# First layer of a four-layer graph network: softmax on 16 steps at once, weighted one-hots, one masking product, and every engine one turn behind the one that feeds it

## The chip, the cores and the metric

One core of one Trainium2 chip runs the whole network in one program. The metric is the device time of one execution in microseconds (us), median of several. A core has TensorE (matrix products; TensorE's weight loads are counted apart), VectorE, ScalarE and GpSimd, a queue SP that issues DMAs, 16 DMA engines, an on-chip memory SBUF and the accumulators of TensorE, PSUM, in 8 banks. The engines run their own instruction streams and wait for each other by semaphores.

## The reference

6250 nodes with 128 features, 100,000 edges sorted by destination, four message-passing layers, each followed by a residual and a layer norm:

```
edge_index = [src, dst]
x = layernorm(x + GAT(x))        # first layer
x = layernorm(x + CF(x, edge_attr_128))
x = layernorm(x + GCN(x))
x = layernorm(x + GIN(x))

GAT:  h = x @ W;  a_s = h @ att_src;  a_d = h @ att_dst      (self-loops are added to the edges)
      e = leaky_relu(a_s[src] + a_d[dst], 0.2)
      e = exp(e - segment_max(e, dst)[dst])
      out = segment_sum(h[src] * e / segment_sum(e)[dst], dst) + bias
CF:   f = ssp(edge @ We1 + be1) @ We2 + be2                   (ssp = softplus - log 2; the edge filter)
      agg = segment_sum((node @ Wn)[dst] * f, src);  node + ssp(agg @ W2 + b2) @ W3 + b3
GCN:  segment_sum(dinv[src] * dinv[dst] * (x @ W.T)[src], dst) + b
GIN:  relu((segment_sum(x[src], dst) + x) @ W1 + b1) @ W2 + b2
```

## The kernel before

The nodes are cut into 49 blocks of 128, the sorted edges into 832 steps of 128, none of which spans two blocks. Four steps (`GRP`) are a turn (a "tick" in the code), so there are 208 turns (`TICKS`). The sum over a step's edges into its block's nodes is a product of a one-hot matrix (edge x place in the block) with the gathered source rows.

The change is in the first layer, whose turns carry three things at once:
- the attention layer itself. GpSimd gathers four times 128 rows of `gat_table` (h and a_s, 130 columns; line 1545) into a ring of `RT` slots of four steps. SP loads the places of the edges as a row, broadcast to all partitions (`places_in`, line 1678). VectorE makes two one-hots, `hot_bf` (edge x place, `gat_hot`, line 663) and `hot_t` (place x edge, `gat_turn`, line 672). TensorE's `gat_mask` (lines 1346, 1349, 1352) adds minus a big number, the one-hot times a big number and the edges' a_s, so that VectorE's row maximum (line 684) gives the maximum of each node over the step. `gat_max` (lines 684 to 718) turns this into a running maximum over the steps of a block and the factor by which the old sums shrink. `gat_pair` (line 1366) brings a_d and the maximum back from nodes to edges by six-column products; `gat_logit` (lines 726 to 739) makes the logits. ScalarE's `gat_weight` takes the exponentials (lines 1097, 1101, 1105) and scales the four one-hots by them (line 1110). `gat_product` (line 1375) sums weighted rows, and `gat_sum` (line 753) adds them to the block's sums. A gather of turn t waits for the product of turn t − `RT` (line 1545's loop).
- the edge filter of the second layer, for 196 of the 208 turns (`FTICKS`): SP loads 512 edges (line 1672), `f_hidden_of` (line 1394) is the first product, `f_soft` the softplus on ScalarE (lines 1122, 1124, 1126), `f_plus_of` its last operation on VectorE (line 761), `f_filter` (lines 1383, 1386) the second product, `f_made_of` (line 1132) the copy that SP writes to `filter_table` (line 1684). The products have one PSUM bank each: bank 0 hidden, bank 1 filter.
- in the background, one or two pieces a turn: the sort that makes the second edge list (lines 419 and 420 on VectorE, `weave` and `background_turns`), and a count on ScalarE (line 997).

The order of the work on each engine is fixed by the program. In turn t an engine handles each part's turn t − lag, in the order of a written list:

```
DVE:  (3, gat_max), (8, gat_sum), (5, gat_logit), (3, f_plus_of), (1, gat_hot), (3, gat_turn)   # woven piece by piece
ACT:  (3, f_soft), (1, gat_dst), (6, gat_weight), (5, f_made_of)
PE:   (7, gat_product), (4, gat_pair), (2, gat_mask), (4, f_filter), (2, f_hidden_of)
```

`f_filter(u)` waits for `f_made_of(u-1)` (bank 1 is free), `f_hidden_of(u)` for `f_plus_of(u-1)` (bank 0 is free), `f_soft(u)` for `f_hidden_of(u)`. The layers behind (`plain_layer`: a one-hot at line 871, a product at 1470, a sum at 859, gathers at 1545) use the same ring of slots. A branch for unsorted edges is in the program and isn't taken with these inputs.

## Time and profile before

| | |
|---|---|
| median of 3 runs | 6158.22 us (6145.17 to 6159.83) |
| the profiled execution's own time | 6132.96 us |
| its span, first to last instruction | 6131.0 us |
| TensorE products / VectorE / ScalarE / GpSimd busy | 2912.4 / 2787.6 / 1397.4 / 3443.1 us |
| mean granted clock of TensorE | 0.661 of full speed |
| turns of the first layer, first to last line 761 | 199.5 to 1689.4 us |
| last sum of the first layer (line 753) starts | 1763.4 us |

All times are from the start of the span of one profiled execution. Busy times are sums of instruction durations without overlap; waits, branches and the issue of DMAs are not counted as busy. An instruction may start before the one ahead of it on its engine has ended, so that the distance of two starts is shorter than a duration. A granted clock of 1.00 is 2.4 GHz, one of 0.50 is 1.2 GHz. The releaser behind an arrow is inferred from semaphore events.

### The profile page before, as it was taken

How to read it: one execution, taken by the hardware profiler on the slowest of the kernel's cores; microseconds unless marked ns; L12 is line 12 of the kernel's file. 1: busy time of each engine (PE TensorE's matmuls, PEld its weight loads, DVE VectorE, ACT ScalarE, POOL GpSimd, SP SyncE). 2: the span in 40 equal slices, each digit the busy share in tenths (PEclk: the TensorE clock that was granted, in tenths of full speed). 3: DMA queues.
4: the chain of work that ended last, by engine and by line, in shares of the span. 5: the costliest groups of instructions: out<-in, count | busy, mean ns of one | idle time of the engine just before them, and what ended most of it. 6: DMA issues, size and time to landing. Idle time of an engine off the chain costs nothing. (4 is left out here: it accounts for less than half of the span.)

```text
span 6131.0 us, 61568 instructions
## 1 busy us (share of the span) xinstructions
PE 2912.4 (48%) x15033; PEld 2354.7 (38%) x15033; DVE 2787.6 (45%) x9204; ACT 1397.4 (23%) x4575; POOL 3443.1 (56%) x3625
## 2 busy tenths in 40 slices
PE   1687777777756553333333353333333223333335
PEld 1455555555556553223232242232323222223223
DVE  2688778786674442333232352233323523333324
ACT  4576555554546662000000020000000000000001
POOL 0555555554522225766666636666666366666673
PEclk8799889888876775555555575555555555555556
DMA  3544444444448884111111111111111311111113
GB/s 68 141 128 129 121 119 129 121 122 112 121 72 257 250 248 125 48 46 47 46 47 47 47 42 46 47 47 47 47 47 46 47 47 47 46 47 46 47 47 44
DMA packets 460089, 517.48 MB, mean 84 GB/s; under 512 B 85627, under 2 KB 358863, under 8 KB 459734
## 3 DMA queue, kind: packets, MB, share of 16 engines
q0 software_dynamic: 131072, 301.89, 19.9%
q1 hardware_dynamic: 325780, 210.91, 12.4%
q8 instruction: 130, 2.13, 0.1%
q14 instruction: 225, 1.84, 0.1%
q10 hardware_dynamic: 2882, 0.70, 0.1%
HBM read 386.68 MB, written 126.50 MB: 84 GB/s over the span
## 5 line engine op out<-in xcount | busy, mean ns | idle before, releaser
L1470 PE MATMUL bank<-arena 128*128 128x128 f32 x4992 | 1204.6, 417 | 2437.5 <-DVE arena L871 1774.6
L1545 POOL DMA_INDIRECT arena<-node_table,pick x1664 | 1614.7, 970 | 896.3 <-issue 485.5
L1470 PEld LDWEIGHTS bank<-arena 128*128 128x128 f32 x4992 | 1033.7, 307 | 2608.2 <-DVE arena L871 1906.8
L859 DVE TENSOR_TENSOR acc<-acc,bank 128x128 f32 x2496 | 719.7, 288 | 2505.6 <-remote 1745.3
L1545 POOL DMA_INDIRECT arena<-gat_table,pick x832 | 857.2, 1030 | 724.0 <-PE bank L1375 505.9
L1545 POOL DMA_INDIRECT arena<-message_table,pick x832 | 806.1, 969 | 373.5 <-issue 241.2
L1159 ACT COPY xt<-bank 128x512 f32<-128x512 f32 (+1 forms) x39 | 21.6, 554 | 2395.4 <-PE bank L1422 2395.4
L871 DVE TENSOR_TENSOR arena<-iota_free,local 128x512 f32<-128x512 f32 x624 | 430.6, 691 | 5.1 <-issue 3.8
L1459 PE MATMUL bank<-arena 128*128 x1664 | 323.7, 373 | 212.7 <-DVE arena L894 206.9
L1459 PEld LDWEIGHTS bank<-arena 128*128 128x128 f32 x1664 | 301.7, 277 | 234.7 <-issue 233.4
L1624 POOL DMA_DIRECT2D message_table<-arena x208 | 114.0, 548 | 402.2 <-DVE arena L894 398.1
L1352 PE MATMUL bank<-ident,arena 128*128 128x128 f32 x1664 | 324.0, 318 | 0.0
L753 DVE SCALAR_TENSOR_TENSOR acc<-acc,s_scale,bank 128x129 f32 x832 | 288.1, 346 | 63.4 <-issue 30.8
L1151 ACT ACTIVATE rstd<-moments,eps_col 128x4 f32<-128x4 f32 (+1 forms) x52 | 15.5, 298 | 1291.7 <-DVE moments L816 1291.5
L1182 ACT ACTIVATE arena<-arena 128x128 bf16<-128x128 f32 x832 | 257.7, 310 | 199.0 <-DVE arena L886 167.7
L1375 PEld LDWEIGHTS bank<-arena 128*128 128x128 f32 x1664 | 240.8, 215 | 140.3 <-issue 139.6
L1352 PEld LDWEIGHTS bank<-ident,arena 128*128 128x128 f32 x1664 | 272.7, 206 | 10.3
L1386 PE MATMUL bank<-w_L_gnn_We,arena 128*128 128x128 f32 x1568 | 269.1, 324 | 0.0
L1110 ACT ACTIVATE arena<-arena,s_weight 128x128 f32<-128x128 bf16 x832 | 266.0, 391 | 0.9 <-remote 0.2
L761 DVE SCALAR_TENSOR_TENSOR arena<-bank,neg_L_gnn_be,arena 128x512 f32<-128x512 f32 x196 | 146.8, 749 | 256.6 <-ACT arena L1126 215.4
L1122 ACT ACTIVATE arena<-bank,c_L_gnn_be 128x512 f32<-128x512 f32 x196 | 135.0, 689 | 554.0 <-PE bank L1394 383.7
L1375 PE MATMUL bank<-arena 128*128 128x129 f32 x1664 | 250.1, 299 | 18.2 <-DVE acc L753 17.2
(225 smaller groups left out, 3997.3 us busy)
## 6 DMA issues: line engine op xcount, KB each, us to landing
arena<-filter_table SPq DMA_DIRECT2D x832, 64.0 KB
message_table<-arena POOLq DMA_DIRECT2D x208, 256.0 KB, 3.9
filter_table<-arena SPq DMA_DIRECT2D x196, 256.0 KB
xt<-edge_cols SPq DMA_DIRECT2D x131, 256.0 KB
arena<-local_rows SPq DMA_DIRECT2D x208, 128.0 KB
arena<-local_rows POOLq DMA_DIRECT2D x52, 512.0 KB, 6.7
arena<-node_table,pick POOLq DMA_INDIRECT x1664
arena<-edge_cols SPq DMA_DIRECT2D x65, 256.0 KB
```

The costliest lines, as they stand in the source:

```text
L753: e.scalar_tensor_tensor(a, a, small["scale"][:, t % 4, s:s + 1], sum_place(t, s), ALU.mult, ALU.add).then_inc(summed, 1)
L761: e.scalar_tensor_tensor(plus[u % 2][:, :], bank[0][:, :], neg_col["L1_gnn_be1"][:, 0:1], magn[u % 2][:, :], ALU.max, ALU.add).then_inc(f_ ...
L859: e.tensor_tensor(a, a, bank[6 + t % 2][:, s * P:(s + 1) * P], ALU.add).then_inc(sums, 1)
L871: e.tensor_tensor(hot[n % 2][:, :, :], iota_free[:, :].unsqueeze(1).to_broadcast([P, GRP, P]), local[which][:, i:i + GRP].unsqueeze(2).to_ ...
L1110: ins = e.activation(hot[t % 2][:, s, :], hot_bf[t % HR][:, s, :], ACT.Copy, scale=weight[:, s:s + 1])
L1182: e.activation(hot_copy[:, :], hot_n[n % 2][:, s * P:(s + 1) * P], ACT.Copy, accum_out=degree_part[:, i:i + 1]).then_inc(degree_added, 1)
L1352: ins = e.matmul(o, gathered[:, slot(t, s), D + 1:D + 2].to_broadcast([P, P]), ident[:, :], start=False, stop=(s == GRP - 1))
L1375: ins = e.matmul(sum_place(t, s), hot[t % 2][:, s, :], gathered[:, slot(t, s), 0:D + 1], start=True, stop=True)
L1386: ins = e.matmul(bank[1][:, s * P:(s + 1) * P], plus[u % 2][:, s * P:(s + 1) * P], mats["L1_gnn_We2"][:, :], start=False, stop=(s == GRP - 1))
L1459: ins = e.matmul(bank[n % 2][:, s * P:(s + 1) * P], hot_n[n % 2][:, s * P:(s + 1) * P], xn[:, bass.ds(b, 1), :].rearrange("p o d -> p (o d ...
L1470: ins = e.matmul(bank[6 + n % 2][:, s * P:(s + 1) * P], hot[n % 2][:, s, :], gathered[:, slot(n, s), 0:D], start=True, stop=True)
L1545: e.indirect_dma_start(out=dst, out_offset=None, in_=table, in_offset=bass.IndirectOffsetOnAxis(ap=index, axis=0)).then_inc(done, 16)
```

## The change

- Softmax in groups of `GT` = 4 turns, 16 steps (`GW`): `gat_max`, `gat_logit`, `gat_pair`, `gat_dst` and the exponentials of `gat_weight` run once in four turns on tiles four times as wide; only the maximum over the mask product stays in every turn (`gat_top`).
- `hot_bf` and ScalarE's scaling are gone. `gat_hot` runs after the exponentials and writes the weighted one-hot by one VectorE operation per step (compare with the place, times the weight).
- The masking product is one of 512 columns, from `hot_t`, in the place of four of 128; `hot_t` has 9 buffers (3 before).
- The filter activation `f_plus_of` writes in place (`magn`; `plus` is gone) and stands last in VectorE's turn, `f_made_of` stands before `f_soft` on ScalarE, and `f_soft(u)` waits for the filter product of turn u − 2 in the place of the filter activation.
- The lags are new, the layer drains in 13 turns (9 before), the ring has 14 slots of a turn (10 before), also for the layers behind.
- Places of the sums and pairs in PSUM are new; small tiles move into the arena; some semaphores are merged.

```diff
-RT = 10
+RT = 14
+GT = 4
+GW = GT * GRP
-SPAN = 16 * GRP
+SPAN = 4 * GW
-HR = 6
+HT = 9
         def sum_place(t, s):
-            return bank[4 + t % 2 + 2 * (s // 3)][:, (s % 3) * (D + 2):(s % 3) * (D + 2) + D + 1]
-        def pair_place(t):
-            return bank[6 + (t + 1) % 2][:, 2 * P:2 * P + 6 * GRP]
+            if s == 0:
+                return bank[6 + t % 2][:, 0:D + 1]
+            return bank[4 + t % 2][:, (s - 1) * (D + 2):(s - 1) * (D + 2) + D + 1]
+        pair_place = bank[6][:, 2 * P:2 * P + 6 * GW]
...
             def gat_turn(t):
                 e.wait_ge(local_row_in[t % 3], 16 * (t // 3 + 1))
-                if t >= 3:
-                    e.wait_ge(paired, t - 2)
+                if t >= HT:
+                    e.wait_ge(paired, (t - HT) // GT + 1)
...
+            def gat_top(t):
+                q = t % GT * GRP
+                e.wait_ge(masked, t + 1)
+                e.tensor_reduce(small["top"][:, t // GT % 2, q:q + GRP],
+                                bank[2][:, :].rearrange("p (s n) -> p s n", s=GRP), AX.X, ALU.max
+                                ).then_inc(max_taken, 1)
+                yield
...
+            def gat_hot(t):
+                g, q = t // GT, t % GT * GRP
+                e.wait_ge(weight_made, g + 1)
+                if t > 1:
+                    e.wait_ge(product_done, t - 1)
+                for s in range(GRP):
+                    i = t * GRP + s
+                    ins = e.tensor_scalar(hot[t % 2][:, s, :], iota_free[:, :], local[0][:, i:i + 1],
+                                          small["weight"][:, g % 2, q + s:q + s + 1], ALU.is_equal, ALU.mult)
+                    if s < GRP - 1:
+                        yield
+                ins.then_inc(hot_weighted, 1)
+                yield
...
             def f_plus_of(u):
                 e.wait_ge(f_log, u + 1)
-                if u > 1:
-                    e.wait_ge(f_done, u - 1)
-                e.scalar_tensor_tensor(plus[u % 2][:, :], bank[0][:, :], neg_col["L1_gnn_be1"][:, 0:1],
+                e.scalar_tensor_tensor(magn[u % 2][:, :], bank[0][:, :], neg_col["L1_gnn_be1"][:, 0:1],
                                        magn[u % 2][:, :], ALU.max, ALU.add).then_inc(f_plus, 1)
...
-            for t in range(TICKS + 9):
-                pieces = []
-                for lag, fn in ((3, gat_max), (8, gat_sum), (5, gat_logit), (3, f_plus_of), (1, gat_hot), (3, gat_turn)):
-                    if 0 <= t - lag < (FTICKS if fn is f_plus_of else TICKS):
+            for t in range(TICKS + 13):
+                pieces = [gat_top(t - 3)] if 0 <= t - 3 < TICKS else []
+                for lag, fn in ((6, gat_max), (8, gat_logit)):
+                    if (t - lag) % GT == 0 and 0 <= t - lag < TICKS:
+                        pieces.append(fn((t - lag) // GT))
+                for lag, fn in ((12, gat_sum), (10, gat_hot), (1, gat_turn)):
+                    if 0 <= t - lag < TICKS:
                         pieces.append(fn(t - lag))
                 weave(pieces, background, background_turns(t))
+                if 0 <= t - 3 < FTICKS:
+                    run(f_plus_of(t - 3))
...
             def gat_weight(t):
-                e.wait_ge(weight_made, t + 1)
-                if t > 1:
-                    e.wait_ge(product_done, t - 1)
-                for s in range(GRP):
-                    ins = e.activation(hot[t % 2][:, s, :], hot_bf[t % HR][:, s, :], ACT.Copy, scale=weight[:, s:s + 1])
-                ins.then_inc(hot_weighted, 1)
...
-                softplus(u, GRP * P, magn, bank[0], "L1_gnn_be1", f_hidden, f_plus, f_log)
+                softplus(u, GRP * P, magn, bank[0], "L1_gnn_be1", f_hidden, f_done, f_log)
...
-                for lag, fn in ((3, f_soft), (1, gat_dst), (6, gat_weight), (5, f_made_of)):
+                for lag, fn in ((4, gat_dst), (9, gat_weight)):
+                    if (t - lag) % GT == 0 and 0 <= t - lag < TICKS:
+                        fn((t - lag) // GT)
+                for lag, fn in ((5, f_made_of), (3, f_soft)):
...
             def gat_mask(t):
-                e.wait_ge(hot_made, t + 1)
+                e.wait_ge(hot_turned, t + 1)
...
                 e.matmul(bk[:, :], neg_big_row[:, :], ones_row[0:1, :], start=True, stop=False)
+                e.matmul(bk[:, :], big_ident[:, :], hot_t[t % HT][:, :], start=False, stop=False)
+                e.wait_ge(ring[t % RT], ring_value("gat", t))
                 for s in range(GRP):
-                    o = bk[:, s * P:(s + 1) * P]
-                    e.matmul(o, hot_bf[t % HR][:, s, :], big_ident[:, :], start=False, stop=False)
-                    if s == 0:
-                        e.wait_ge(ring[t % RT], ring_value("gat", t))
...
-                for lag, fn in ((7, gat_product), (4, gat_pair), (2, gat_mask), (4, f_filter), (2, f_hidden_of)):
+                if (t - 7) % GT == 0 and 0 <= t - 7 < TICKS:
+                    gat_pair((t - 7) // GT)
+                for lag, fn in ((11, gat_product), (2, gat_mask), (4, f_filter), (2, f_hidden_of)):
```

## Rows read from the trace of the kernel before

**Rows 1.** Busy time of each engine (x instructions) in three stretches; start:end, length first.

```profile
199.50:1689.50 1490.00, 1149.75 (x7117) 849.33 (x7117) 1163.68 (x4444) 865.95 (x2437) 804.29 (x780) 0.90 0.45 122
...
1689.50:1764.00 74.50, 50.94 (x346) 43.09 (x344) 59.76 (x284) 29.94 (x125) 26.21 (x27) 0.81 0.59 58
...
3626.00:4821.00 1195.00, 405.09 (x1664) 347.71 (x1664) 360.45 (x1035) 0.00 (x0) 808.96 (x832) 0.54 0.21 46
```

**Rows 2.** Line 761: count, ns min/median/max, first and last start us.

```profile
L761 DVE SCALAR_TENSOR_TENSOR arena<-bank,neg_L_gnn_be,arena x196: 736/751/754, 199.5 to 1689.4; 128x512 f32<-128x512 f32 x196
```

**Rows 3.** Order of time: start us, us, engine, line; one turn of the first layer.

```profile
911.23 0.69 ACT L1122 ACTIVATE arena<-bank,c_L_gnn_be 128x512 f32<-128x512 f32 x1 [2.50 <-issue]
...
912.61 0.63 ACT L1126 ACTIVATE arena<-arena 128x512 f32<-128x512 f32 x1
...
913.28 0.75 DVE L761 SCALAR_TENSOR_TENSOR arena<-bank,neg_L_gnn_be,arena 128x512 f32<-128x512 f32 x1 [0.42 <-ACT arena L1126]
...
913.70 1.28 ACT L1110 ACTIVATE arena<-arena,s_weight 128x128 f32<-128x128 bf16 x4
...
914.89 0.56 ACT L1132 COPY arena<-bank 128x512 f32<-128x512 f32 x1
...
915.59 0.37 PE L1383 MATMUL bank<-filter_parts,ones_row 3*128 3x512 bf16 x1 [1.14 <-ACT arena L1132]
...
916.89 1.02 PE L1394 MATMUL bank<-xt,w_L_gnn_We 128*128 128x512 f32 x2
...
917.95 0.69 ACT L1122 ACTIVATE arena<-bank,c_L_gnn_be 128x512 f32<-128x512 f32 x1 [2.50 <-issue]
```

**Rows 4.** Waits from 300 to 1700 us: total us, times, longest us.

```profile
POOL arena L1545 <- PE bank L1375: 467.3, 181, 15.0
...
ACT arena L1122 <- PE bank L1394: 357.0, 111, 9.8
...
PE bank L1383 <- ACT arena L1132: 196.7, 140, 11.3
...
DVE arena L761 <- ACT arena L1126: 180.3, 82, 16.0
```

**Rows 5.** The view of Rows 1, of single turns and of the last six.

```profile
897.90:906.50 8.60, 6.45 (x26) 4.60 (x24) 4.79 (x21) 4.03 (x13) 2.82 (x4) 0.60 0.40 107
...
906.50:913.30 6.80, 5.50 (x41) 4.13 (x41) 6.07 (x24) 4.20 (x15) 4.87 (x5) 1.00 0.43 137
...
1648.70:1689.50 40.80, 30.37 (x218) 23.28 (x218) 29.46 (x128) 24.87 (x74) 22.72 (x24) 1.00 0.49 124
```

**Rows 6.** Groups of instructions, 300 to 2000 us: count, busy us, mean ns, idle before.

```profile
L753 DVE SCALAR_TENSOR_TENSOR acc<-acc,s_scale,bank 128x129 f32 x797 | 276.0, 346 | 60.6 <-issue 29.6 <-PE bank L1375 6.2 <-ACT s_scale L1105 2.8
...
L663 DVE TENSOR_TENSOR arena<-iota_free,local 128x512 bf16<-128x512 f32 x192 | 131.0, 682 | 0.0
...
L837 DVE TENSOR_TENSOR arena<-x_sb,r_L_gnn_bias 128x512 f32<-128x512 f32 x12 | 8.1, 677 | 0.0
```

**Rows 7.** Order of time on VectorE: a small-op stretch, and four scalings after the layer.

```profile
909.29 0.18 DVE L688 TENSOR_TENSOR s_logit<-s_top,arena 128x4 f32<-128x4 f32 x1
911.82 0.68 DVE L684 TENSOR_REDUCE s_top<-bank 128x4 f32<-128x512 f32 x1
...
1770.74 1.08 DVE L822 TENSOR_SCALAR x_sb<-arena,moments,rstd 128x128 f32<-128x128 f32 x4
```

**Rows 8.** Groups, as Rows 6: TensorE's masking product, GpSimd's gathers.

```profile
L1349 PE MATMUL bank<-big_ident,arena 128*128 128x128 bf16 x772 | 176.2, 228 | 0.0
...
L1545 POOL DMA_INDIRECT arena<-gat_table,pick x752 | 773.5, 1029 | 648.4 <-PE bank L1375 468.6 <-issue 172.3 <-remote 7.6
```

**Rows 9.** Waits of GpSimd from 2470 to 6060 us, as Rows 4.

```profile
POOL arena L1545 <- remote: 365.2, 113, 7.9
```

**Rows 10.** Order of time in the third layer, around one such wait.

```profile
4604.77 0.29 DVE L859 TENSOR_TENSOR acc<-acc,bank 128x128 f32 x1 [15.28 <-remote]
...
4604.89 0.94 POOL L1545 DMA_INDIRECT arena<-node_table,pick  x1 [3.33 <-remote]
```

More of the change, by code:

```diff
@@ L37 @@
 EPS = 1e-5
[L38 removed]
+RT = 14
+GT = 4
+GW = GT * GRP
 RING = RT * GRP
[L40 to L41 removed]
+SPAN = 4 * GW
+ARENA_WORDS = 30056
 BAD_SRC = 8000
@@ L252, in build_program @@
         magn = [part([P, GRP * P]) for _ in range(2)]
-        plus = [part([P, GRP * P]) for _ in range(2)]
         filters = [part([P, GRP, D]) for _ in range(2)]
@@ L674, in gat_turn @@
                 yield
-            def gat_max(t):
-                i, r, c = t * GRP, t % 4, t * GRP % SPAN
-                top, logit, new, old, drop = (small[n][:, r, :] for n in ("top", "logit", "new", "old", "drop"))
-                before, now = parts[:, 0, 1, c:c + GRP], parts[:, 0, 1, c + 1:c + 1 + GRP]
-                if t and c == 0:
-                    e.wait_ge(drop_made, t)
-                    own(e.tensor_copy(parts[:, 0, 1, 0:1], parts[:, 0, 1, SPAN:SPAN + 1]))
+            def gat_top(t):
+                q = t % GT * GRP
@@ L693, in gat_max @@
                 after(q)
-                q = own(e.tensor_tensor(new, new, self_max[:, i:i + GRP], ALU.max))
+                q = own(e.tensor_tensor(new, new, self_max[:, i:i + GW], ALU.max))
                 yield
                 after(q)
-                if t >= SPAN // GRP:
-                    e.wait_ge(paired, t - SPAN // GRP + 1)
-                q = own(e.tensor_tensor_scan(now, same[:, i:i + GRP], new, before[:, 0:1], ALU.add, ALU.max))
+                if g >= SPAN // GW:
+                    e.wait_ge(paired, g - SPAN // GW + 1)
@@ L700, in gat_max @@
+                q = own(e.tensor_tensor_scan(now, same[:, i:i + GW], new, before[:, 0:1], ALU.add, ALU.max))
                 yield
                 after(q)
[L702 to L704 removed]
+                e.wait_ge(dst_put, g + 1)
+                q = own(e.tensor_tensor(parts[:, 1, :, c + 1:c + 1 + GW], parts[:, 0, :, c + 1:c + 1 + GW],
+                                        upper[:, 0, :, c + 1:c + 1 + GW], ALU.subtract))
```

199 lines of the change are left out of this document (98 added, 101 removed).

## The prediction

> **What bounds the kernel now.** I read first the busy time by stretch [rows 1]. The turns of the first layer run from the first to the last filter activation on VectorE, line 761, 196 of them [rows 2]: 1490 us for 195 intervals, 7.64 us a turn, and another 74.5 us until the last sum. In that stretch TensorE is busy 1150 us (5.90 a turn), VectorE 1164 (5.97), ScalarE 866 (4.44), GpSimd 804 (4.12). Nobody is full, so something alternates. The order of time of one turn shows what [rows 3]: ScalarE works without a gap from 911.23 to 915.45 (softplus 2.0 us, then the small exponentials and the four scalings of the one-hots, then the filter copy L1132); only then may TensorE start the filter product L1383, and behind it in its own order stands the hidden product L1394, which ends at 917.91; only then may ScalarE start its next softplus at 917.95. 4.22 us of ScalarE and 2.46 us of TensorE in series are 6.7 us. The waits say the same: TensorE L1383 for L1132 197 us, ScalarE L1122 for L1394 357 us, VectorE L761 for ScalarE 180 us; GpSimd waits 467 us for products, so it is not the bound either [rows 4]. The check is the stretch in which the background sort is over: VectorE has only 29.5 us of work in 40.8 us there, and the six turns still take 6.8 us each at a clock of 1.00 [rows 5]. The rest, from 6.8 to 7.64, is turns in which TensorE's clock was granted at 1.2 GHz part of the time (8.6 us at 0.60 against 6.8 at 1.00 [rows 5]; mean 0.90 [rows 1]) and a few long waits, the longest 16.0 us [rows 4].
>
> **The alternation goes.** ScalarE now copies the filter before its softplus, the one-hots leave it (1.28 us a turn [rows 3]), and the filter product needs only things of the turn before. What is left as a loop from turn to turn: L761 releases the hidden product (1.02), that the softplus (911.23 to 913.24, 2.0), that the next L761 (0.75), with hand-overs about 4.0 us [rows 3]. L761 now stands last in VectorE's turn, so VectorE does its other work inside this loop. 4.0 is below the engines' own work, so the bound becomes the busiest engine.
>
> **VectorE's turn.** From 5.97 us:
> - the bf16 one-hot L663 goes: 0.68, of which some 0.08 overlaps its neighbour, −0.60 [rows 6];
> - the softmax runs once for 16 steps. Its small instructions take 909.29 to 911.82 less three sums at 0.26 each, 1.75 us, and with the pair reduction 1.9 us a turn [rows 7]. A quarter is 0.47. They are 12 elements wider; by 512 elements in 677 ns against 4 in 0.18 us an element costs about 1 ns [rows 6, 7], so a dozen of them add some 0.2 us per four turns, double-width ones included. New: 0.6, −1.3;
> - the weighted one-hots come: four two-scalar operations of 128x128, which the trace has in the same form at 1.08 us for four back to back [rows 7], +1.05. Bounds: 0.25 each hidden behind the sums, 0.35 each alone (the sum L753 [rows 6]), 1.0 to 1.4.
> That is 5.1 us (5.1 to 5.5) with background. One turn in four carries ten small operations more, another four more, one in five a second sort step.
>
> **TensorE's turn.** At full clock 30.4 us for six turns, 5.06 us [rows 5]. The mask's four bf16 products of 0.23, of which 0.11 shows [rows 8], become one of 512 columns, −0.2. The pair products are the same number, moved into one turn in four: those turns are some 0.75 us longer, and their mask reaches VectorE that much later. 4.9 us at full clock; at 1.2 GHz a turn is near 9. With 18% of the time at the low level as now, n·9 and m·5.6 average 6.0; with none 5.6.
>
> **GpSimd's turn.** A gather is 1.029 us and 0.305 of issue (172.3 over some 565), four are 5.34 us [rows 8]. Now 1.5 to 2 us of waiting hide behind that; after the change nothing does. It is the hardest floor: 195 x 5.34.
> The Trainium skill, SBUF — State Buffer, "Who interferes with whom", speaks against this change: VectorE in a two-port mode and GpSimd exclude each other for a whole instruction, and scalar-operand operations on SBUF data are of that kind. What it would add is the second rival's mechanism; it does not enter the sum.
>
> **Waits that are added.** VectorE's top reduction waits for the mask product of the turn before, with everything of that turn queued behind it. TensorE needs hidden 1.1, product 1.1, mask 1.6 and gaps, 4.3 us after the last L761, in pair turns 5.1: late against a short VectorE turn by up to 0.5, one turn in four, 0.1 on average. The gathered rows may run only 5 turns ahead of the mask before and after (10 slots less 5, 14 less 9). SP's row of places is now needed two turns sooner, at lag 1 and not 3. It is issued when the turn two back has hidden its edges, so two turns, over 10 us, remain; only where the sort's last steps make SP wait does its landing show, perhaps 20 us once. The filter's write-out must land within about 4 us more than a turn; it cost nothing but the one long wait of 16 us. The moved small tiles and merged semaphores cost nothing: same instructions.
>
> **The sum.** Floor 5.34 (GpSimd), VectorE 5.1 with uneven turns, TensorE 4.9 to 6.0 by its clock. Three engines this close don't average perfectly: I take 5.9, and 0.1 for the long waits, which stay: 6.0 us. 195 x (7.64 − 6.0) = 320 us gained. The pipeline is four turns deeper: 13 turns of drain and not 9, each without filter work and mostly empty, +5 us. The layers behind keep their instructions; their ring of slots grows from 10 to 14. GpSimd waits 365 us there [rows 9] in which the ring was full: VectorE had had nothing for 15.3 us, then sums, and 0.1 us later GpSimd goes on [rows 10]. A deeper ring could give anything between 0 and all of it. But the 832 gathers of a layer take 1195 us though GpSimd needs 1.25 each (0.95 and 0.30 [rows 10]), and the ring is full again every few turns, which looks like a rate of landing, not a single delay: I take 0. So −315 on the profiled execution's 6132.96 gives 5818. The runs' median is 6158.22, 25 above it: **5843 us** as the median, own range 5740 to 5940 (turns of 5.5 to 6.5).
>
> **Rivals.**
> 1. The deeper ring also frees the later layers (23%). For: every one of the 113 waits is short, 3.2 us on average [rows 9], and four more turns are 20 us of cover. Against: the landing lag fills whatever is given. Half of the 365 us: 5660; all: 5480.
> 2. GpSimd or the clock holds the turn (22%). If every gather meets one of the new scalings and waits its 0.33 us out, GpSimd's turn is 5.34 + 1.34 = 6.7 us. For: gathers at 1.029 us mean against 0.95 in rows 10 show that VectorE's work already lengthens them. Against: the long two-input one-hot L663 goes at the same time. Time: −183 + 5, 5980. A colder TensorE gives the same: at a clock of 0.75 its turn is about 6.6.
>  By the Trainium skill, TensorE: Matmul & The Clock Gate, Part 1, the clock falls after idleness and rises with sustained work; the 8.6 us turn [rows 5] follows a long wait, which agrees, and by this rule the denser TensorE would stay at 2.4 GHz, turn 5.6, 5765 us.
> 3. Slower: landing of the gathers (6%). In the later layers the wait of rows 10 is for the product ten turns back, so landings lag some 50 us there. If GpSimd, once it issues without pause in the first layer too, meets this lag, with five turns ahead the turn is 50/5 = 10 us: +460, 6620. It decides from a lag of 38 us (5 x 7.64) on. Against: the view of rows 4 lists no mask product that waits for a gather; but GpSimd pauses in every turn there.
> 4. No gain (3%): the filter write-out, now ahead of the softplus in ScalarE's order, ties the turn to its landing; 7.6 us a turn, 6160.
>
> **Chances.** Forecast 46%. A measurement here tells 0.3%, 18 us, from nothing. Faster 0.91 (forecast, rivals 1 and 2), same 0.03, slower 0.06. The range reaches into rival 1 to its half and over rival 2: 5610 to 6050.
>
> **What would show it.** Right: 195 intervals of the filter activation at 5.6 to 6.3 us; ScalarE under 3.2 us a turn, with waits; the weighted one-hots at 0.33 us each with starts 0.26 apart; TensorE's first product of a turn no longer waiting for the filter copy; GpSimd over 85% of the turn. Wrong: gathers above 1.2 us (rival 2), mask products waiting for gathers (rival 3), the later layers below 1150 us each (rival 1), a granted clock under 0.85.

## The result, and the profile after

Changed kernel 5987.8 us (5972.9 to 5995.9, 4 runs), kernel before in the same session 6159.0 (6145.2 to 6161.8, 4 runs): ratio 0.9724, 95% interval 0.9699 to 0.9748. The forecast was 5843, with 5740 to 5940 around it and 5610 to 6050 with the rivals: the sign holds, the time lies in the wide range and not in the narrow one, and the gain is a little over half of the one forecast. The profiled execution took 5989.27 us, its span is 5987.5: 143.5 less than before.

Where that is: the line of the filter activation (774 now) answers to [rows 2], and the last sum (768) to the end of the loop in [rows 1].

```profile
L774 DVE SCALAR_TENSOR_TENSOR arena<-bank,neg_L_gnn_be,arena x196: 733/746/756, 195.0 to 1485.6; 128x512 f32<-128x512 f32 x196
...
L768 DVE SCALAR_TENSOR_TENSOR acc<-acc,arena,bank x832: 317/342/357, 256.9 to 1568.0; 128x129 f32 x167
```

195 intervals in 1290.6 us are **6.62 us a turn** (7.64 before, 6.0 forecast). The last sum starts 195 us sooner than before. So the first layer gained 195 us, and some 52 were given back behind it. The busy time of the engines in the loop and in its drain, in the view of [rows 1]:

```profile
195.00:1485.60 1290.60, 1061.80 (x6389) 782.24 (x6486) 1015.13 (x3103) 581.36 (x1090) 815.37 (x779) 0.90 0.58 140
1485.60:1568.00 82.40, 59.69 (x351) 49.77 (x354) 59.70 (x225) 3.61 (x17) 25.76 (x28) 0.73 0.48 42
```

A turn holds 5.21 us of VectorE, 5.45 of TensorE, 2.98 of ScalarE and 4.18 of GpSimd, and the granted clock is where it was, 0.90. Nobody is full: there are waits that [rows 4] did not list (300 to 1500 us: total, times, longest):

```profile
ACT arena L1144 <- remote: 222.8, 37, 16.3
POOL arena L1560 <- PE bank L1388: 189.3, 84, 14.1
...
ACT arena L1144 <- DMA filter_table<-arena: 133.2, 65, 15.3
...
ACT arena L1144 <- PE bank L1399: 73.5, 38, 4.9
DVE arena L669 <- remote: 70.9, 26, 9.6
```

L1144 is ScalarE's filter copy, now ahead of the softplus. It waits 65 times for the write-out of the copy two turns back, 38 times for TensorE's filter product (L1399), and 37 times, for 223 us, for something that this view calls "remote". The trace also keeps the time of every semaphore event that it recorded, and they tell what: all 37 waits end within 0.03 us of the event by which TensorE reports its filter product done, none with a landing. The 26 waits of the top reduction L669 end in the same way with TensorE's report of the mask product. The order of time shows one of the long ones ("SPq" is the issue of a transfer by SyncE):

```profile
1042.57 0.59 ACT L1144 COPY arena<-bank 128x512 f32<-128x512 f32 x1 [1.83 <-DMA filter_table<-arena]
...
1043.88 0.43 SPq L1699 DMA_DIRECT2D filter_table<-arena  x1
...
1046.14 1.16 PE L1399 MATMUL bank<-w_L_gnn_We,arena 128*128 128x128 f32 x8
...
1051.86 0.69 DVE L669 TENSOR_REDUCE arena<-bank 128x4 f32<-128x512 f32 x1 [3.33 <-remote]
...
1055.50 0.59 ACT L1144 COPY arena<-bank 128x512 f32<-128x512 f32 x1 [9.97 <-remote]
1055.53 0.33 SPq L1687 DMA_DIRECT2D xt<-edge_cols  x1
```

The copy at 1055.50 needs two things. The write-out issued at 1043.88 (of the copy before the one shown) had landed long before: its last packet ends at 1046.75. The filter product ends at 1047.30 by its rows, but its event comes at 1055.47, 8.2 us later. Over the whole layer the last packet of a write-out ends 3.0 us after the issue in the median and 6.7 us at most. In the middle of the layer 27 turns have over 8 us between a write-out's issue and the copy that needs it; in none of them does the copy's wait end with a landing.

Such late reports are what is new in this layer. While its gathers run, the trace has 650 events of TensorE's products, and 237 of them come more than 1 us, up to 17 us, after the recorded end of the product; in the kernel before it is 31 of 852, and behind the layer's last gather none in either kernel. (On this chip the trace lacks part of the events while gathers run.) Whether the product itself or only its report is late can't be told, since the ends of products are modelled. Copy to copy, 32 turns of the middle 169 in which the copy waited for a late report take 9.74 us on average, the other 137 take 5.84.

The later layers have the same instructions in both kernels, and their ring is deeper. The last gather of the second of them and its last sum:

```profile
4626.86 0.98 POOL L1560 DMA_INDIRECT arena<-node_table,pick  x1 [0.30 <-issue]
...
4661.20 0.29 DVE L877 TENSOR_TENSOR acc<-acc,bank 128x128 f32 x1 [0.15 <-DVE acc L877]
```

34.3 us lie between them; in the three layers 34.4, 34.3 and 34.6, where the kernel before had 17.5, 21.9 and 25.3 (counted from its order of time). From the start of a turn's last gather to the start of its last sum it is now 72 us in the median, before 48. Each layer is 18 to 21 us longer, 57 in all: 39 of them are the longer ends, and 18 a slower run of the gathers (1180 to 1181 us a layer, before 1173 to 1176). GpSimd still waits for a free slot, 400 us over the three layers in place of 376: the ring is deeper, the queue behind it is longer, and nothing comes sooner.

What the queue waits for is not the landing. In both kernels the last packet of a gather ends 2.2 us after the start of its issue in the median and 13.4 us at most. The last packet of this layer's gathers ends at 4638.5. From then on next to nothing moves, and TensorE and VectorE work off rows that have all arrived (in the view of [rows 1]):

```profile
4640.00:4661.00 21.00, 16.27 (x69) 13.72 (x68) 15.06 (x45) 0.00 (x0) 0.00 (x0) 0.58 0.01 1
```

Before that VectorE's sums wait for TensorE's product. Over the three layers (2163 to 5931 us):

```profile
DVE acc L877 <- remote: 1861.2, 242, 20.2
```

All 242 waits end with TensorE's report of the product L1485. Of 426 such events recorded while gathers run, 248 come over 1 us after the product's recorded end, up to 17.9 us; in the kernel before it is 245 of 433. So the consumer is late, and a deeper ring only lets GpSimd run further ahead of it.

### The profile page after: what moved, and what is told of

Same layout as the page of the kernel before. It is cut to its first block and busy times, and to the rows that moved or that the text cites. A ratio compares the mean times of both kernels' runs of the same rounds, so it can differ in the third digit from the quotient of the medians.

```text
span 5987.5 us, 55573 instructions
## 1 busy us (share of the span) xinstructions
PE 2830.5 (47%) x14308; PEld 2292.2 (38%) x14409; DVE 2636.6 (44%) x7807; ACT 1087.4 (18%) x3119; POOL 3450.6 (58%) x3625
## 5 line engine op out<-in xcount | busy, mean ns | idle before, releaser
L1485 PE MATMUL bank<-arena 128*128 128x128 f32 x4992 | 1208.4, 418 | 2487.6 <-DVE arena L889 1745.2
L1485 PEld LDWEIGHTS bank<-arena 128*128 128x128 f32 x4992 | 1037.5, 308 | 2658.5 <-DVE arena L889 1871.3
L1560 POOL DMA_INDIRECT arena<-gat_table,pick x832 | 869.4, 1045 | 511.9 <-PE bank L1388 224.5
L768 DVE SCALAR_TENSOR_TENSOR acc<-acc,arena,bank 128x129 f32 x832 | 283.9, 341 | 29.4 <-issue 24.2
L749 DVE TENSOR_SCALAR arena<-iota_free,local,arena 128x128 f32<-128x128 f32 x832 | 291.6, 351 | 0.1
L1365 PE MATMUL bank<-ident,arena 128*128 128x128 f32 x1664 | 241.5, 292 | 20.4 <-issue 19.3
L1399 PE MATMUL bank<-w_L_gnn_We,arena 128*128 128x128 f32 x1568 | 248.9, 306 | 1.2 <-issue 1.2
L1365 PEld LDWEIGHTS bank<-ident,arena 128*128 128x128 f32 x1664 | 242.7, 209 | 8.4 <-issue 1.4
L1399 PEld LDWEIGHTS bank<-w_L_gnn_We,arena 128*128 128x128 f32 x1568 | 209.3, 207 | 51.2 <-issue 51.2
L904 DVE TENSOR_SCALAR arena<-arena,iota_part 128x512 f32<-128x512 bf16 x208 | 101.3, 487 | 274.2 <-DMA arena<-local_rows 195.5
```

What stands on the lines that cost most here:

```text
L749: ins = e.tensor_scalar(hot[t % 2][:, s, :], iota_free[:, :], local[0][:, i:i + 1], small["weight"][:, g % 2, q + s:q + s + 1], ALU.is_equ ...
L768: e.scalar_tensor_tensor(a, a, small["scale"][:, g % 2, q + s:q + s + 1], sum_place(t, s), ALU.mult, ALU.add).then_inc(summed, 1)
L1365: ins = e.matmul(bk[:, s * P:(s + 1) * P], gathered[:, slot(t, s), D + 1:D + 2].to_broadcast([P, P]), ident[:, :], start=False, stop=(s == ...
L1399: ins = e.matmul(bank[1][:, s * P:(s + 1) * P], magn[u % 2][:, s * P:(s + 1) * P], mats["L1_gnn_We2"][:, :], start=False, stop=(s == GRP - 1))
L1485: ins = e.matmul(bank[6 + n % 2][:, s * P:(s + 1) * P], hot[n % 2][:, s, :], gathered[:, slot(n, s), 0:D], start=True, stop=True)
L1560: e.indirect_dma_start(out=dst, out_offset=None, in_=table, in_offset=bass.IndirectOffsetOnAxis(ap=index, axis=0)).then_inc(done, 16)
```

## The experiments

They ran in four sessions on three chips, and on all three the kernel before takes 5664 to 5687 us and not 6159. Which chip the first session had is not on record; I call it the first chip, but that the chip and not something else of that session made the difference is not shown. Each session has its own runs of the kernel before, so the ratio is what compares across sessions. "Turn" is the interval of the filter activation, from the first and last start of its 196 instructions.

```
kernel                      turn    median us   before   ratio (95%)
after (first session)       6.62     5987.8     6159.0   0.9724 (0.9699-0.9748)
e9  before, unchanged       7.46     5664.1     5680.1   one run
e5  changed, unchanged      5.73     5357.5     5687.4   0.9426 (0.9407-0.9445)
e2  later layers 10 ahead   5.81     5351.9     5668.7   0.9432 (0.9411-0.9453)
e3  later layers 4 ahead    5.82     5352.4     5668.7   0.9430 (0.9407-0.9452)
e1  third filter buffer     5.74     5362.6     5668.7   0.9456 (0.9431-0.9481)
e8  write-out first         5.76     5356.2     5687.4   0.9412 (0.9387-0.9437)
e11 write-out twice         5.99     5381.8     5680.1   0.9476 (0.9447-0.9506)
e7  old ScalarE order       5.75     5346.2     5687.4   0.9396 (0.9381-0.9412)
e10 scalings on ScalarE     5.69     5339.9     5680.1   0.9415 (0.9387-0.9442)
e12 e7 and e10 together     6.79     5541.8     5677.9   0.9762 (0.9734-0.9790)
e4  before, new order       9.44     6051.0     5668.7   1.0673 (1.0646-1.0699)
e6  e4, write-out first     7.09     5592.5     5687.4   0.9831 (0.9814-0.9847)
```

### The two kernels on another chip: e5 and e9

No edit; the changed kernel and the kernel before.

> The changed kernel as it is, as the control for e1 to e4 and e6 to e8. Theory (a gather's landing rate differs from chip to chip, and only where it is low is anything but VectorE the bound): on a chip where the kernel before takes about 5670 us this takes 5350 to 5370 (ratio 0.944, turns of 5.8 us), the same as e2 and e3 within 10 us, since the ring's depth is never used there; on a chip where the kernel before takes 6160 it takes 5990 (0.972). Rival (the turns ahead matter on every chip): on the first kind of chip it differs from e2 and e3 by over 20 us.

> The kernel before as it is, for its trace on the kind of chip on which it takes 5670 to 5690 us and the changed kernel 5357. Theory (two savings of such a chip are apart: gathers land promptly, so each later layer takes about 1055 us instead of 1195, 420 us in three; and the first layer's alternation hardly changes): turn 7.2 to 7.5 us, later layers 1045 to 1060, so the change's gain is the first layer's alone, 195 x (7.35 - 5.73) = 315. Rival (the first layer of the kernel before was slowed by landings too): turn below 7.0 us. On a chip where it takes 6160 the trace is that of rows 1 to 10 again.

The filter activation of e9 and of e5, as above:

```profile
L761 DVE SCALAR_TENSOR_TENSOR arena<-bank,neg_L_gnn_be,arena x196: 736/751/753, 198.8 to 1653.0; 128x512 f32<-128x512 f32 x196
```

```profile
L774 DVE SCALAR_TENSOR_TENSOR arena<-bank,neg_L_gnn_be,arena x196: 732/743/752, 199.8 to 1316.7; 128x512 f32<-128x512 f32 x196
```

7.46 and 5.73 us: here the change is worth 1.73 us a turn, 337 in all, against 1.02 on the first chip. What differs between the chips shows in the page's row of the rate of transfer in 40 slices, here that of the changed kernel on the first chip and then of e5:

```profile
GB/s 70 154 144 148 142 138 146 146 128 141 60 255 252 252 139 44 46 46 47 45 47 47 34 50 46 47 46 46 46 46 44 47 44 47 46 46 46 47 46 41
```

```profile
GB/s 74 162 167 161 160 160 156 163 146 173 45 256 254 251 234 53 53 53 53 52 51 52 43 57 53 53 53 53 53 53 52 49 53 53 53 53 52 53 53 50
```

In the later layers, which are gathers and little else, 46 to 47 against 53, and in the plain copies between (slices 12 to 14) the same 251 to 256. In e5 a turn's last sum follows its last gather by 6.2 us in the median, not 72, and GpSimd never waits for a slot: its 832 gathers take 1038 to 1051 us, 1.25 each, which is its own issue. On the first chip the same gathers take 1173 to 1181, some 5.65 us for a turn's four, whichever the ring.

The numbers expected of e5 and e9 came, but for one later layer of e9 (1065 us); the cause behind them, a gather's rate of landing, did not. Gathers land as promptly on the first chip, 2.2 us in the median on both in the later layers; they are fewer in a microsecond because GpSimd waits for slots, and the slots for products. What differs is TensorE's reports. The sums' wait of the later layers in e5 (1998 to 5290 us) has TensorE's name on it, and the waits are short:

```profile
DVE acc L877 <- PE bank L1485: 1786.5, 624, 10.4
```

In the traces of all twelve runs on the other chips no report of a product comes more than 0.05 us after the product's recorded end. On the first chip the share that comes over 1 us late grows with the rate of gathers: 4% with four in 7.64 us (first layer, before), 36% with four in 6.62 (first layer, after), 57 to 58% with four in 5.65 (later layers, both), none in a first layer behind its last gather. Why TensorE is late there, and only while gathers run, no run tells.

### The ring of the later layers: e2 and e3

```
-                    if t >= RT:
-                        e.wait_ge(plain_product, base + t - RT + 1)
+                    if t >= 10:          # e3: 4
+                        e.wait_ge(plain_product, base + t - 10 + 1)
```

> The changed kernel, but in the three later layers GpSimd may run only 10 turns ahead, as before the change (the first layer keeps its 14 slots). Theory: these layers are bound by the rate at which gathers land, so a deeper ring only makes the lag longer and each layer's drain with it: 34 us from last gather to last sum in the changed kernel, 18 to 25 before. Expected 3 x 18 = 54 us less than the changed kernel, about 5935 us, each later layer back at 1194 to 1198 us. Rival: the longer drain is by chance or by the start, no change within 10 us.

> The changed kernel, but in the three later layers GpSimd may run only 4 turns ahead. If landing is bound by a rate, the lag shrinks to about 15 to 20 us, the 1180 us from first to last gather stay, and the drain falls from 34 to some 10 us: about 70 us less than the changed kernel, 5915 us. If instead each landing takes a fixed 40 us or more however few are out, four turns in 40 us are 10 us a turn and the three layers take 2080 us each: over 8500 us. If back-to-back issue by GpSimd is itself what delays landings, the waits break it up and the layers come out below 1180 us: under 5850 us.

With 4, 10 or 14 turns ahead the time is the same within 6 us, and each later layer takes 1049 to 1057 us from first gather to last sum; e9, whose ring has 10, takes 1045 to 1065. Where TensorE is prompt depth is worth nothing, and neither expectation, both written for the first chip, was put to its test. Where TensorE is late, depth could not be varied: no later session met that. That the 57 us are the deeper ring's doing there rests on the two traces of the first session alone, and for the 18 us of slower gathers even the way is not shown.

### The write-out on ScalarE's path: e4, e6, e1, e8, e11

e4, the kernel before with ScalarE's new order alone:

```
-                for lag, fn in ((3, f_soft), (1, gat_dst), (6, gat_weight), (5, f_made_of)):
+                for lag, fn in ((5, f_made_of), (3, f_soft), (1, gat_dst), (6, gat_weight)):
```

> The kernel before with one edit: ScalarE's order in a turn is filter copy, softplus, then the small exponentials and the scalings, so that the filter product no longer waits for ScalarE's whole turn. Theory of the prediction: the alternation of ScalarE and TensorE was the bound, so this alone takes most of the gain: VectorE, at 5.97 us a turn with uneven turns, and the clock are next, 6.6 to 6.9 us a turn in place of 7.64, 5955 to 6010 us, with the later layers unchanged. Rival: the gain of the change needs the lighter VectorE and TensorE and the wider distances between engines; then the turn stays over 7.3 us and the time over 6090 us.

It is 7% slower than the kernel before, 9.44 us a turn. Its order of time tells all of it:

```profile
903.37 0.59 ACT L1132 COPY arena<-bank 128x512 f32<-128x512 f32 x1 [0.28 <-DMA filter_table<-arena]
903.85 0.69 ACT L1122 ACTIVATE arena<-bank,c_L_gnn_be 128x512 f32<-128x512 f32 x1
...
905.90 0.75 DVE L761 SCALAR_TENSOR_TENSOR arena<-bank,neg_L_gnn_be,arena 128x512 f32<-128x512 f32 x1 [2.07 <-ACT arena L1126]
...
907.17 0.35 DVE L672 TENSOR_SCALAR arena<-arena,iota_part 128x512 bf16<-128x512 bf16 x1
...
907.54 0.32 SPq L1678 DMA_DIRECT2D arena<-local_rows  x1
907.91 0.43 SPq L1672 DMA_DIRECT2D arena<-edge_cols  x1
...
908.38 0.44 SPq L1684 DMA_DIRECT2D filter_table<-arena  x1
...
913.00 0.59 ACT L1132 COPY arena<-bank 128x512 f32<-128x512 f32 x1 [5.39 <-DMA filter_table<-arena]
```

SyncE issues in one order: the row of places, which needs VectorE's L672 of that turn, then the edges, then the write-out of the copy made a turn earlier. So a copy's write-out goes out one turn and 5.0 us after the copy starts (907.17 is 3.8 behind 903.37, three issues follow), the copy two turns on needs it and starts 4.3 us later in the median, 4.6 here (913.00 less 908.38): 2T = T + 5.0 + 4.5, T = 9.5. Measured 9.44. In the kernel before the copy stands last in ScalarE's turn, 3.7 us later [rows 3], behind the softplus; there it only has to come before the next filter product, and its wait for the landing lies in the shade of the alternation.

e6 is e4 with the write-out first in SyncE's turn:

```
+                if 0 <= t - 6 < FTICKS:
+                    filters_out(t - 6)
                 if t < TICKS:
                     places_in(t)
                 if t < FTICKS:
                     edges_in(t)
-                if 0 <= t - 6 < FTICKS:
-                    filters_out(t - 6)
```

> The kernel before with two edits and no others: ScalarE copies the filter before its softplus (as in e4), and SyncE issues the filter's write-out ahead of that turn's rows of places and edges instead of behind them. e4, with the first edit alone, took 9.44 us a turn. Theory A (the write-out's place in SyncE's order ties e4's turn: copy to issue 14.4 us, of it one whole turn, and 4.4 us of landing make two turns, so T = 5.0 + 4.4): issued a turn earlier, the loop allows 4.7 us, and the turn becomes that of VectorE and TensorE with the low clock, 6.3 us (6.0 to 6.8); time of the kernel before less 195 x (7.5 - 6.3), ratio 0.95 to 0.97. Rival B (ScalarE's order itself is bad for the old kernel, since the one-hots' weights then come after the softplus and the product late): the turn stays above 8.5 us, ratio over 1.03.

The loop opens, 9.44 becomes 7.09, and the wait for the landing is gone from its waits. So e4's loop was the one described. But 6.0 to 6.8 was expected, and the gain over the kernel before is 1.7%, not 3 to 5. Its busy time in 1000 us, as [rows 1]:

```profile
300.00:1300.00 1000.00, 832.78 (x5137) 602.17 (x5138) 851.61 (x3230) 637.38 (x1766) 588.40 (x560) 0.91 0.48 130
```

VectorE is at 85%, TensorE at 83% at a clock of 0.91. The order alone takes 0.37 us off the old turn. The waits show the next loop, TensorE's product waiting for VectorE's sum and its mask for VectorE's row maximum, 1.0 us a turn together; how much of the 7.09 it holds was not taken apart.

```profile
PE bank L1375 <- DVE acc L753: 81.8, 97, 1.8
...
PE bank L1346 <- DVE s_top L684: 60.5, 106, 1.0
```

In the changed kernel places wait for an operation two turns further ahead, and SyncE waits in its place for the hidden product of the turn before: copy to issue is then 4.9 us at least, 7.0 in the median of e5 (softplus, filter activation, hidden product and the edges' issue stand between), and no turn besides. The loop asks for T = (4.9 + landing) / 2; with e5's 3.9 us from issue to copy in the median that is 4.4 us, and with the longest landing of the first chip, 6.7, it is 5.8. That is what e1, e8 and e11 try. e1 adds a third buffer to copy into (and takes two of the nine transposed one-hots for its room); e8 makes e6's edit in the changed kernel; e11 writes every copy out twice:

```
 def filters_out(u):
     ...
+    e.dma_start(message_table[u * GRP * P:(u + 1) * GRP * P, :].rearrange("(s p) d -> p s d", p=P),
+                filters[u % 2][:, :, :]).then_inc(f_out[u % 2], 16)
```

> The changed kernel with a third buffer for the filter copy (the place-by-node one-hots have 7 buffers in place of 9 to make room). Theory: in the changed kernel ScalarE's copy L1144 waits for the landing of the write-out two turns back (356 us in the list of waits by that and by an unknown queue), and that delays softplus, the filter activation and with it VectorE; with a third buffer these waits go and the turn falls from 6.62 us to about 6.1, some 100 us less than the changed kernel, near 5890 us. Rival: the landings are late for everybody, gathers too, and the mask product takes the wait over; then half of it or less, 5940 to 5990 us. Second rival: the engines' own uneven turns and the clock are the bound, no change (5970 to 5995 us).

> The changed kernel with the filter's write-out first in SyncE's turn, ahead of the rows of places and the edges, so that it is issued right behind the copy and not 4 to 5 us later, behind the hidden product. Theory A (the filter copy waits for the write-out's landing in a third to a half of the turns): with fast landings as e1, the third buffer: 5 to 20 us under e5; where the kernel before takes 6160 and landings of 8 to 11 us are common, turns of 6.6 us become 6.1 to 6.3, 60 to 100 us under e5. Rival B (the landing itself is slow because of the gathers' traffic, and then all of SyncE's transfers are late, edges and rows of places too): the copy no longer waits, but the time is that of e5 within 10 us, with waits for edges or rows of places in its place.

> The changed kernel with the filter's write-out doubled: a second transfer of the same 256 KB goes to a table that is overwritten later, behind the first, and the copy two turns later waits for both. It doubles the suspected cost (the landing) and nothing else of the path. Theory A (copy to issue 5.0 us and landing 4.4 us make two turns: 4.7 us, below the engines' 5.6; a landing of 7 to 8 us makes it 6.0 to 6.5): turn 6.0 to 6.5 us, 60 to 140 us over e5, with the waits of ScalarE L1144 for filter_table in most turns. Rival B (the landing is not on the path, the engines' turn hides it): within 20 us of e5.

The waits of ScalarE's copy from 300 to 1300 us, in e5, in e8 and in e11:

```profile
ACT arena L1144 <- DMA filter_table<-arena: 155.0, 70, 15.8
ACT arena L1144 <- PE bank L1399: 127.0, 86, 4.4
```

```profile
ACT arena L1144 <- PE bank L1399: 230.8, 151, 5.3
...
ACT arena L1144 <- DMA filter_table<-arena: 22.6, 3, 14.6
```

```profile
ACT arena L1144 <- DMA message_table<-arena: 372.7, 133, 17.2
```

In e8 the copy's wait for the landing is down to 3 times, and it waits longer for TensorE's filter product instead; the turn does not move, and in e1 neither. So on these chips the landing ends many of the copy's waits but costs no time. e11 more than doubles the wait and adds 0.26 us a turn, 24 us over e5 by the medians, 0.5% by the ratios, whose intervals lie just apart: a small price, under half of the least expected. The second transfer does not double the landing, either: the last packet of the pair ends 4.8 us after the first issue in the median, against 3.1 for the one of e5.

These runs were to explain the first chip too, but there the write-outs land no later (3.0 us in the median, 6.7 at most; in e5 3.1 and 7.0), and the copy waits no longer for them (133 us in 1200, in e5 155 in 1000). So the 0.9 us by which the first chip's turn is longer is not the write-out's. The 32 turns with a late report of TensorE (9.74 us against 5.84) make 0.74 of it. That is read from one trace; no run made TensorE prompt there, or late elsewhere.

### What gave the gain: e7, e10, e12

e7 puts ScalarE's old order back into the changed kernel: softplus, small tiles, copy. e10 puts the scalings back on ScalarE, last in its turn, and VectorE makes plain one-hots in one operation. e12 does both.

```
 # e7
+                if 0 <= t - 3 < FTICKS:
+                    f_soft(t - 3)
                 for lag, fn in ((4, gat_dst), (9, gat_weight)):
                     ...
-                for lag, fn in ((5, f_made_of), (3, f_soft)):
-                    ...
+                if 0 <= t - 5 < FTICKS:
+                    f_made_of(t - 5)
 # e10
-                    ins = e.tensor_scalar(hot[t % 2][:, s, :], iota_free[:, :], local[0][:, i:i + 1],
-                                          small["weight"][:, g % 2, q + s:q + s + 1], ALU.is_equal, ALU.mult)
+                e.tensor_tensor(hot[t % 2][:, :, :], iota_free[:, :].unsqueeze(1).to_broadcast([P, GRP, P]),
+                                local[0][:, i:i + GRP].unsqueeze(2).to_broadcast([P, GRP, P]), ALU.is_equal)
+                ...
+                    ins = e.activation(hot[t % 2][:, s, :], hot[t % 2][:, s, :], ACT.Copy,
+                                       scale=small["weight"][:, g % 2, q + s:q + s + 1])
```

> The changed kernel with ScalarE's order put back: softplus, then the small tiles, then the filter copy. Theory A (the alternation is short once the one-hots and the small tiles have left ScalarE: softplus 2.0, copy 0.6, filter and hidden product 2.5, hand-overs 0.3, 5.4 us at full clock and over 7 at the low one): turn 6.0 to 6.4 us against 5.8 of e5 on a fast-landing chip, +40 to +110 us. Rival B (the order is what brought the gain): the turn goes back to 7 us and more, +230 us or more. Rival C (the write-out's landing is what holds the changed kernel, and the old order gives it time): no loss or a gain.

> The changed kernel with one part undone: VectorE makes the one-hots unweighted, one operation of 512 elements instead of four weighted ones of 128 (0.69 us against 1.05), and ScalarE scales them last in its turn, 4 x 0.32 = 1.28 us, as in the kernel before. Theory A (VectorE's work is the bound of the changed kernel on a promptly landing chip, and ScalarE with 2.95 us of a 5.75 us turn has room): turn 5.4 us, 50 to 80 us under e5's 5357, ratio 0.93. Rival B (ScalarE's scalings stand between its softplus and the next copy, and the alternation of ScalarE and TensorE comes back: copy 0.6, softplus 2.0, scalings 1.3, then filter and hidden product 2.5): turn 6.2 to 6.6, 90 to 170 us over e5. Rival C (GpSimd's floor of 5.34 plus waits, or TensorE, holds it): within 15 us of e5.

> The changed kernel with ScalarE's turn as it was in the kernel before, except that the small exponentials come every fourth turn: softplus, small tiles, scalings of the one-hots, and then the filter copy. It joins the edits of e7 (order) and e10 (scalings), each of which alone left the time where it was. Theory A (the alternation is what bounded the kernel before, and either edit alone is enough to break it: with both undone ScalarE works 2.0 + 1.3 + 0.6 us and TensorE's filter and hidden product 2.5 us in series again, 6.4 us and hand-overs, more at the low clock): turn 6.6 to 7.1 us, 160 to 260 us over e5, ratio 0.97 to 0.99. Rival B (the alternation was not the bound; fewer small operations and the turns of distance between the engines did it): turn 5.7 to 5.9 us, within 20 us of e5, ratio 0.94. Rival C (both share it): turn 6.0 to 6.4 us.

e7: 5.75, no loss at all (ratio 0.9396 against 0.9426, the intervals touch). The alternation is still in its waits, as theory A had it, but it is short enough to hide (300 to 1300 us, 174 turns; L1134 is the softplus, L1408 and L1397 the hidden and the first filter product):

```profile
ACT arena L1134 <- PE bank L1408: 428.5, 158, 5.1
...
PE bank L1397 <- ACT arena L1144: 70.1, 129, 10.1
```

e10: 5.69, no loss either, though ScalarE works 4.1 us a turn; and no clear gain, though VectorE works 4.92 us and not 5.17 (959 and 1007 us over 195 turns). So VectorE alone did not bound e5; GpSimd's floor is as near. e12: 6.79, 1.06 us a turn, 184 us over e5 by the medians, all as its theory A said. Its waits from 300 to 1300 us, and those of e9, the kernel before (L1129 is the softplus and L1139 the copy in e12, L1414 and L1403 are the hidden and the first filter product):

```profile
ACT arena L1129 <- PE bank L1414: 345.0, 131, 4.5
...
PE bank L1403 <- ACT arena L1139: 199.5, 146, 2.3
DVE arena L769 <- ACT arena L1133: 161.9, 103, 6.4
```

```profile
ACT arena L1122 <- PE bank L1394: 328.6, 123, 5.9
...
PE bank L1383 <- ACT arena L1132: 130.8, 116, 2.1
DVE arena L761 <- ACT arena L1126: 113.1, 79, 4.7
```

The same three waits: the alternation is back. One turn of it, to hold against [rows 3]:

```profile
902.23 0.69 ACT L1129 ACTIVATE arena<-bank,c_L_gnn_be 128x512 f32<-128x512 f32 x1 [2.50 <-PE bank L1414]
...
904.61 1.26 ACT L1146 ACTIVATE arena<-arena 128x128 f32<-128x128 f32 x4
905.77 0.56 ACT L1139 COPY arena<-bank 128x512 f32<-128x512 f32 x1
906.48 0.37 PE L1403 MATMUL bank<-filter_parts,ones_row 3*128 3x512 bf16 x1 [1.86 <-ACT arena L1139]
...
909.30 0.69 ACT L1129 ACTIVATE arena<-bank,c_L_gnn_be 128x512 f32<-128x512 f32 x1 [2.97 <-PE bank L1414]
```

ScalarE without a gap from 902.23 to 906.33, TensorE from 906.48 to the next softplus: 7.07 us. The old alternation with a batched softmax costs 6.79; relieve it on either side, by the order or by the scalings, and the turn falls to about the engines' own work. Of the 1.73 us between e9 and e5, 1.06 come back when the alternation alone is put back, and 0.67 are the rest of the change. The parts don't simply add up: in the kernel before, the order alone gave 0.37 (e6), since other loops stood close behind.

## Why the prediction was right or wrong

1. **The bound of the kernel before**, ScalarE and TensorE in series: right, and shown by e12, at 6.79 us with the small tiles made once for four turns. Other bounds stood close behind it, as e6 shows with 7.09. That *both* edits were needed to lift it was my reading, and is wrong: with the rest of the change in place each alone is enough (e7, e10).
2. **VectorE 5.1 us** (5.1 to 5.5): measured 5.21, and 5.17 in e5. The weighted one-hots took 0.34 us in the median and started 0.26 behind their neighbours, as forecast.
3. **TensorE 4.9 us at full clock**: 5.03 in e5 at 0.98 (980.46 over 195). On the first chip the clock stayed at 0.90, as I had carried over. By the Trainium skill, TensorE: Matmul & The Clock Gate, Part 1, a denser TensorE keeps its high level: from 300 to 1300 us e9 has 0.92 and e5 0.98, which agrees; on the first chip it stayed at 0.90 though TensorE was busier (5.45 us of 6.62, before 5.90 of 7.64), which does not. The wait ahead of the 8.6 us turn's fall in clock, which the second rival calls long, was 2.2 us (897.9 to 900.2).
4. **GpSimd's floor, 5.34 us**: in e5 four gathers of 1.068 and four issues of 0.288 make 5.42, 95% of the turn; "over 85%" held there, on the first chip it was 82% (4 x 1.046 and 4 x 0.305 of 6.62). It is the nearest floor of the new turn, and e10, in which a lighter VectorE gains nothing clear, fits that; no run lowered it. By the Trainium skill, SBUF — State Buffer, "Who interferes with whom", the weighted one-hots can lock GpSimd out for their length; gathers took 1.040 us in e9, 1.068 in e5, and 1.023 in e10 and 1.048 in e12, where those one-hots are gone: the traces agree with the direction, and the price is 0.02 to 0.045 us a gather, not the third of a microsecond of rival 2.
5. **The turn, 6.0 us**: this is the term that was mis-sized, 6.62 on the chip of the forecast (+121 us) and 5.73 on the others. The step that failed is "I take 5.9, and 0.1 for the long waits, which stay". They did not stay: on that chip TensorE's reports came over 1 us late 237 times in 650, before 31 in 852, and ScalarE's copy alone waited 223 us for them in 300 to 1500. By the turns with and without such a wait they cost some 0.74 us a turn, not 0.1. Nothing in the trace of the kernel before pointed to that but the unnamed waits of its later layers, which I read as landings. Why the denser layer makes TensorE late stays open. The filter's write-out, for which a condition was given in the prediction and a whole turn in rival 4, met the condition: it landed in 6.7 us at most. That it can cost more than the gain, in another order of SyncE, is shown by e4.
6. **The lag of the gathers**, rival 3: ten microseconds a turn did not come, and its premise does not hold. The wait of [rows 10] is for a product ten turns back, but the rows themselves land 2.2 us after the issue (13.4 at most), not 50. The measured 5988 lies next to rival 2's 5980 by luck: gathers did not become longer (1.046 us, not 1.36), and the clock stayed at 0.90.
7. **Drain +5 us**: +8 on the first chip (82.4 for 74.5), +15 on the others (84.9 from e5's last activation to its last sum, 70.2 in e9).
8. **The later layers, 0**: rival 1 hoped for up to 365 us, the traces say +57 on the first chip and nothing on the others (three layers of e9 sum to 3165 us, of e5 to 3170). A rate and not a single delay it was, but TensorE's and not the landing's; and I took from it that depth is free. It lengthens the lag, and a layer ends with its lag.

Together: −315 forecast, −143.5 measured. Of the difference of 171.5, 121 is the turn, 57 the later layers, 3 the drain, against which stand 4.5 of an earlier start and 5 unplaced. On the chips of the experiments the span fell by 317 us (5662.0 in e9, 5344.9 in e5), the forecast's 315: a coincidence in part, since there the turn was 0.27 shorter and the old turn 0.18 shorter than in the sum.

## What to carry to other kernels

Before an instruction is moved ahead in an engine's order, work out its loop with each transfer that it waits for: where the issue stands in its own queue, how many turns of buffer lie between, and T = (copy to issue + landing) / buffers, with the landing taken at its worst, not its median. Two engines in series are cut by shortening either side, so undo parts one by one and then together, or both look worthless. A ring that is full because its consumer is slow gains nothing from more slots, and here paid for them at each layer's end. And a wait that the profile can't name is not yet a late transfer: compare its end with the semaphores' events and with the last packet of the transfer, before a theory is built on it.

## What the runs showed of the hardware

- Two kinds of session: in the first, on one chip, the kernel before took 6159 us and a later layer 1194 to 1216, in the later ones, on three chips, 5664 to 5687 and 1045 to 1080. Transfers were alike on both: plain copies at 250 GB/s; a gather of 128 rows in the later layers landed 2.2 us after the start of its issue in the median, 14 at most; a write-out of 256 KB beside the gathers landed in 3.0 and 3.1 us (the changed kernel on the two kinds) and in 4.0 (the kernel before on both).
- What differed was TensorE: in the first session, and but for one event of 1.2 us only while GpSimd's gathers ran, its semaphore events came up to 18 us after the recorded end of the product, in 4% of the cases with four gathers in 7.64 us and in 57% with four in 5.65. In the later sessions none came over 0.05 us late.
- A tuned kernel's gain depended on that: 2.8% in the first session, 5.7% in the later ones (e5).
